# A relational graph layer: the first group of tiles in pairs, an earlier weight load, and the window table built in steps 1 to 3

## The reference

```python
h = relu(layernorm(x))                          # no gain, eps 1e-5
W_rel = einsum('rb,bdf->rdf', w_comp, weight)   # 32 types from 8 bases of 128 x 128
agg = segment_sum(h[src] * norm, etype * N + dst, R * N).reshape(R, N, D)
out = x + relu(einsum('rnd,rdf->nf', agg, W_rel) + h_bias + h @ loop_weight)
```

## Time and profile before

| | before |
|---|---|
| median of 3 runs | 1015.2 us |
| profiled execution | 1015.24 us |
| span of that execution | 1013.5 us |
| PE busy | 990.3 us (98%) |
| DVE busy | 955.0 us (94%) |
| ACT busy | 884.6 us (87%) |
| POOL busy | 723.8 us (71%) |
| mean granted clock of PE | 0.999 |

### The profile page before, as it was taken

One profiled execution on the slowest core, in us unless ns is written; L12 is line 12 of the kernel. 1 busy time (PEld: TensorE's weight loads), 2 busy tenths in 40 slices (PEclk: granted clock), 3 DMA queues, 4 the chain that ended last, 5 costly groups with the idle time before them and its releaser, 6 DMA issues.

```text
span 1013.5 us, 23775 instructions
## 1 busy us (share of the span) xinstructions
PE 990.3 (98%) x4902; PEld 574.4 (57%) x4902; DVE 955.0 (94%) x4366; ACT 884.6 (87%) x3242; POOL 723.8 (71%) x1282
## 2 busy tenths in 40 slices
PE   5899999999999999999999999999999999999996
PEld 2355555555556565656565555555555655555655
DVE  6999999999999999999999999999999999999995
ACT  6898989898888889898989898989898988889884
POOL 6877777777777777777777777777777777777740
PEclk9999999999999999999999999999999999999999
DMA  4556555556556555565565555465655655555544
GB/s 116 145 135 165 149 156 164 156 144 169 143 152 173 140 154 161 152 166 155 143 173 141 154 162 158 138 178 140 168 152 152 166 148 155 159 155 141 156 123 140
DMA packets 178223, 154.47 MB, mean 152 GB/s; under 512 B 17781, under 2 KB 151213, under 8 KB 178077
## 3 DMA queue, kind: packets, MB, share of 16 engines
q1 hardware_dynamic: 157261, 101.40, 35.6%
q0 software_dynamic: 20384, 51.32, 19.7%
q10 hardware_dynamic: 432, 0.22, 0.1%
HBM read 101.31 MB, written 51.56 MB: 151 GB/s over the span
## 4 chain that ended last, share of the span: by engine, by line
PE 93%; DVE 2%; POOL 2%; issue 1%; ACT 1%; DMA 1%; DVEq 0%; ACTq 0%; POOLq 0%
PE y_ps L790 33%; PE y_ps L797 31%; PE win_ps L812 9%; PE win_ps L807 8%; PE hT_ps L876 4%; PE hT_ps L803 4%; PE mix_ps L868 1%; POOL xg L578 1%; DVE sum_a L1019 1%; DVE sum_b L1019 0%; DMA xg<-x,idx 0%; DVE msg L1052 0%; PE y_ps L812 0%; DMA src_all<-src 0%; PE y_ps L807 0%
## 5 line engine op out<-in xcount | busy, mean ns | idle before, releaser
L578 POOL DMA_INDIRECT xg<-x,idx x392 | 382.0, 974 | 73.4 <-issue 34.0
L790 PE MATMUL y_ps<-w_all,hT 128*128 128x512 f32 x784 | 412.3, 608 | 2.9 <-DVE sum_a L1019 2.7
L797 PE MATMUL y_ps<-w_all,hT 128*128 128x512 f32 x784 | 400.3, 592 | 0.0
L523 POOL TENSOR_TENSOR u<-z 128x128 f32<-128x128 f32 x392 | 180.4, 460 | 182.8 <-ACT z L626 178.9
L626 ACT ACTIVATE z<-y_ps,mix 128x128 f32<-128x128 f32 x784 | 244.5, 366 | 44.8 <-PE y_ps L797 37.8
L1019 DVE SCALAR_TENSOR_TENSOR sum_b<-y_ps,mix,sum_b 128x128 f32<-128x128 f32 x784 | 265.8, 339 | 0.0
L797 PEld LDWEIGHTS y_ps<-w_all,hT 128*128 128x128 f32 x784 | 149.1, 190 | 187.9 <-issue 164.0
L790 PEld LDWEIGHTS y_ps<-w_all,hT 128*128 128x128 f32 x784 | 132.3, 189 | 119.1 <-DVE sum_a L1019 60.9
L622 ACT ACTIVATE z<-y_ps,mix 128x128 f32<-128x128 f32 x392 | 140.8, 359 | 63.6 <-issue 44.9
L660 ACT ACTIVATE hw<-xw,shift,nrstd 128x128 f32<-128x128 f32 x391 | 192.6, 494 | 0.4 <-DVE shift L1121 0.4
L1019 DVE SCALAR_TENSOR_TENSOR sum_b<-y_ps,mix,z 128x128 f32<-128x128 f32 x392 | 131.4, 335 | 36.1 <-issue 32.3
(11 more groups left out here) (107 smaller groups left out, 1174.3 us busy)
## 6 DMA issues: line engine op xcount, KB each, us to landing
seg<-msgs SPq DMA_DIRECT2D x391, 104.8 KB
msgs<-msg SPq DMA_DIRECT2D x98, 258.0 KB
xw<-x POOLq DMA_DIRECT2D x97, 256.0 KB
out<-res SPq DMA_DIRECT2D x97, 256.0 KB
xg<-x,idx POOLq DMA_INDIRECT x392
type_bc<-type_rows SPq DMA_DIRECT2D x52, 112.0 KB
w_all<-weight SPq DMA_DIRECT2D x1, 512.0 KB
type_bc<-type_rows SPq DMA_DIRECT2D x4, 80.0 KB
```

What stands on the lines that cost most here:

```text
L523: nc.gpsimd.tensor_tensor(u[:, r, :], z[:, r, 0, :], z[:, r, 1, :], ALU.add).then_inc(s_u, 1)
L578: nc.gpsimd.indirect_dma_start(xg[:, q, j, :], None, x, bass.IndirectOffsetOnAxis(ap=idx[:, q, j:j + 1], axis=0)).then_inc(s_gather[q * G ...
L790: nc.tensor.matmul(y_ps[2 * t % 5][:, :, :], hT[:, q, j, :], w_all[:, B // 2:B, :], start=True, stop=True).then_inc(s_y_high, 1)
L797: nc.tensor.matmul(y_ps[(2 * t + 1) % 5][:, :, :], hT[:, q, j, :], w_all[:, 0:B // 2, :], start=True, stop=True).then_inc(s_y, 1)
```

## The change

Group 0: each tile gets its negated mean at once (`s_mean_first` counts tiles). ACT computes three signs, applies relu to tiles 0 and 1, waits for their two transposes and copies them (`s_hT_first`, `s_hT_sb_first`), then comes the fourth sign, and relu of tiles 2 and 3, and a copy of these two. PE runs `first_tiles` within step 0: two transposes, the products of tile 0, two transposes, the products of tile 1; step 1 then begins with tile 2. The other four signs stand in ACT's steps 1 and 2, two in each.

Counts and table: `bin_counts(0)` stands at the head of DVE's step 1 and `bin_counts(1)` at the head of its step 3. `count_bins` is one sequence of eight matmuls in PE's step 3, after the products of the group's second tile. `row_table` stands in DVE's step 3, after the last slot and ahead of the next one-hot.

Loads: `w_all` is issued right after the first types, without a wait. The rest of `src_all` is issued after gather 3 has landed, ahead of `norm_all`, `dst_c` and the types.

```diff
--- before.py
+++ after.py
@@ -50,6 +50,8 @@
 SUMS_AT = 6
 OUT_AT = 5
 LATE = 4
+TABLE_STEP = 3
+PAIR = 2
 LAST_LOADS = 2
 MODE_STORE = 52
 SPAN = 8
@@ -268,6 +270,8 @@
         s_first_hot = sem("s_first_hot")
         s_bn_first = sem("s_bn_first")
         s_mean_first = sem("s_mean_first")
+        s_hT_first = sem("s_hT_first")
+        s_hT_sb_first = sem("s_hT_sb_first")
         s_dst = sem("s_dst")
         s_dst_c = sem("s_dst_c")
         s_consts = sem("s_consts")
@@ -391,10 +395,9 @@
             sp.dma_start(src_all[:, 0:FIRST], src[:, 0:FIRST]).then_inc(s_src_first, 16)
             sp.dma_start(norm_all[:, 0:FIRST], norm[:, 0:FIRST]).then_inc(s_norm_first, 16)
             load_type_rows(0, 0, 2, 0, s_types_first)
-            sp.dma_start(src_all[:, FIRST:NT], src[:, FIRST:NT]).then_inc(s_src, 16)
-            sp.wait_ge(s_gather[1], 16)
             sp.dma_start(w_all[:, :, :], weight.rearrange("b d f -> d b f")).then_inc(s_all, 16)
             sp.wait_ge(s_gather[G - 1], 16)
+            sp.dma_start(src_all[:, FIRST:NT], src[:, FIRST:NT]).then_inc(s_src, 16)
             sp.dma_start(norm_all[:, FIRST:NT], norm[:, FIRST:NT]).then_inc(s_norm, 16)
             sp.dma_start(dst_c[:, :], dst_cols).then_inc(s_dst_c, 16)
             load_types(0)
@@ -627,6 +630,10 @@
                 ins.then_inc(s_z, 1)
 
 
+            def sign(k):
+                nc.scalar.activation(signs[:, k, :], dst_f[:, :], ACT.Sign, bias=limits[:, k:k + 1], scale=-1.0,
+                                     accum_out=below_sum[:, k:k + 1]).then_inc(s_below, 1)
+
             def group_means(g, n, q):
                 if not is_before(g, RING):
                     act.wait_ge(s_hT, g - (RING - 1))
@@ -674,6 +681,10 @@
                 def mixing(j):
                     if 1 <= g <= NG:
                         scale_bases(g - 1, (q - 1) % RING, j)
+
+                def late_sign(i):
+                    if is_before(g, TABLE_STEP):
+                        sign(SPAN // 2 + 2 * (g - 1) + i)
 
                 def normalised(tiles):
 
@@ -702,6 +713,7 @@
                     window_std(g - STD_AT)
                 window(0)
                 mixing(1)
+                late_sign(0)
                 if here:
                     normalised(range(G // 2, G))
                 if node_group(g, TURN_AT) is not None:
@@ -717,6 +729,7 @@
                 if not beyond(g, NG - 1):
                     group_means(g + 1, round_after(n, q), (q + 1) % RING)
                 mixing(3)
+                late_sign(1)
                 if not beyond(g, NG - 1):
                     group_squares(g + 1, (q + 1) % RING)
                 window(3)
@@ -727,26 +740,24 @@
             act.wait_ge(s_consts, 1)
             nc.scalar.activation(root[:, :], eps_col[:, :], ACT.Sqrt)
             act.wait_ge(s_limits, 1)
-            def sign(k):
-                nc.scalar.activation(signs[:, k, :], dst_f[:, :], ACT.Sign, bias=limits[:, k:k + 1], scale=-1.0,
-                                     accum_out=below_sum[:, k:k + 1]).then_inc(s_below, 1)
-
             def first_relu(j):
                 nc.scalar.activation(h[:, 0, j, :], xg[:, 0, j, :], ACT.Relu, bias=neg_mean[:, 0, j:j + 1]).then_inc(s_relu, 1)
 
-            for k in range(SPAN - 2):
+            for k in range(SPAN // 2 - 1):
                 sign(k)
-            act.wait_ge(s_mean_first, 1)
-            first_relu(0)
-            first_relu(1)
-            sign(SPAN - 2)
-            sign(SPAN - 1)
+            for j in range(PAIR):
+                act.wait_ge(s_mean_first, j + 1)
+                first_relu(j)
+            act.wait_ge(s_hT_first, 1)
+            nc.scalar.activation(hT[:, 0, 0:PAIR, :], hT_ps[:, 0:PAIR, :], ACT.Copy).then_inc(s_hT_sb_first, 1)
+            sign(SPAN // 2 - 1)
+            act.wait_ge(s_mean_first, PAIR + 1)
+            first_relu(PAIR)
             act.wait_ge(s_mean, 1)
-            first_relu(2)
-            first_relu(3)
+            first_relu(G - 1)
             nc.scalar.activation(std[:, 0, :], nmv[:, NRING - 1, :, 1], ACT.Sqrt, bias=eps_col[:, 0:1]).then_inc(s_std, 1)
             act.wait_ge(s_hT, 1)
-            nc.scalar.activation(hT[:, 0, :, :], hT_ps[:, :, :], ACT.Copy).then_inc(s_hT_sb, 1)
+            nc.scalar.activation(hT[:, 0, PAIR:G, :], hT_ps[:, PAIR:G, :], ACT.Copy).then_inc(s_hT_sb, 1)
             group_means(1, 0, 1)
             group_squares(1, 1)
             sweep(act, STEPS, step, first=1)
@@ -771,15 +782,14 @@
         @block.tensor
         def _(pe):
 
-            def count_bins(half):
+            def count_bins():
                 counts = win_ps[0:1, :, :].rearrange("p b f -> p (b f)")
                 pe.wait_ge(s_first_hot, 1)
-                pe.wait_ge(s_bins, half + 1)
-                for k in range(half * (SPAN // 2), (half + 1) * (SPAN // 2)):
+                pe.wait_ge(s_bins, 2)
+                for k in range(SPAN):
                     mm = nc.tensor.matmul(counts[:, 0:BINS], in_bin16[:, k:k + 1], first_hot[:, SPAN - k:SPAN - k + BINS],
                                           start=k == 0, stop=k == SPAN - 1)
-                if half == 1:
-                    mm.then_inc(s_hist, 1)
+                mm.then_inc(s_hist, 1)
 
             pe.wait_ge(s_weights, 16)
 
@@ -838,16 +848,16 @@
 
             def step(g, n, q):
                 def messages(j):
-                    if 1 <= g <= NG:
-                        if j == 0:
+                    if 1 <= g <= NG and not (is_before(g, 2) and j < PAIR):
+                        if j == (PAIR if is_before(g, 2) else 0):
                             pe.wait_ge(s_hT_sb, g)
-                        if g == 1 and j == 0:
-                            pe.wait_ge(s_all, 16)
                         product_high(g - 1, (q - 1) % RING, j)
                         product_low(g - 1, (q - 1) % RING, j)
 
                 messages(0)
                 messages(1)
+                if g == TABLE_STEP:
+                    count_bins()
                 if node_group(g, TURN_AT) is not None:
                     window_transposes(g - TURN_AT)
                 if node_group(g, SUMS_AT) is not None:
@@ -868,7 +878,8 @@
                     nc.tensor.matmul(mix_ps[:, P:P + G * B], hotT[:, q, :], w_mix[:, :],
                                      start=True, stop=True).then_inc(s_mix_ps, 1)
                     if is_before(g, 1):
-                        count_bins(0)
+                        first_tiles()
+                        return
                     pe.wait_ge(s_relu, g * G + G)
                     if node_group(g, TURN_AT) is not None:
                         pe.wait_ge(n_hT_sb, g - TURN_AT + 1)
@@ -877,8 +888,24 @@
                     mm.then_inc(s_hT, 1)
                 messages(3)
 
+            def first_tiles():
+
+                for j in range(PAIR):
+                    pe.wait_ge(s_relu, j + 1)
+                    mm = nc.tensor.transpose(hT_ps[:, j, :], h[:, 0, j, :], ident[:, :])
+                mm.then_inc(s_hT_first, 1)
+                pe.wait_ge(s_hT_sb_first, 1)
+                pe.wait_ge(s_all, 16)
+                product_high(0, 0, 0)
+                product_low(0, 0, 0)
+                for j in range(PAIR, G):
+                    pe.wait_ge(s_relu, j + 1)
+                    mm = nc.tensor.transpose(hT_ps[:, j, :], h[:, 0, j, :], ident[:, :])
+                mm.then_inc(s_hT, 1)
+                product_high(0, 0, 1)
+                product_low(0, 0, 1)
+
             step(0, 0, 0)
-            count_bins(1)
             sweep(pe, STEPS, step, first=1)
 
             pe.wait_ge(s_table, 16)
@@ -1154,6 +1181,10 @@
                     if k is not None and j < windows_of(k):
                         window_stats(k, j)
 
+                if g == 1:
+                    bin_counts(0)
+                if g == TABLE_STEP:
+                    bin_counts(1)
                 tile_slot(g, n, q, 0, more)
                 stats_of(0)
                 tile_slot(g, n, q, 1, more)
@@ -1186,6 +1217,8 @@
                     window_rstd(g - STD_AT)
                 tile_slot(g, n, q, 3, False)
                 stats_of(3)
+                if g == TABLE_STEP:
+                    row_table()
                 if more:
                     one_hot(g + 1, (q + 1) % RING)
                 if node_group(g, STD_AT) is not None:
@@ -1204,17 +1237,12 @@
                 nc.vector.bn_stats(nstats[:, NRING - 1, j, :], xg[:, 0, j, :]).then_inc(done, 1)
                 dve.wait_ge(done, 2 * (j % DV) + 1)
                 nc.vector.bn_aggr(nmv[:, NRING - 1, j, :], nstats[:, NRING - 1, j, :]).then_inc(done, 1)
+                dve.wait_ge(done, 2 * (j % DV) + 2)
+                nc.vector.tensor_scalar(neg_mean[:, 0, j:j + 1], nmv[:, NRING - 1, j, 0:1], -1.0, None,
+                                        ALU.mult).then_inc(s_mean_first if j < G - 1 else s_mean, 1)
                 if j == 1:
-                    dve.wait_ge(s_bn, 2 * DV)
```

(7 more changed lines are left out.)

## The result

| | before | after |
|---|---|---|
| median, runs of one comparison | 1015.62 us (8 runs) | 1019.58 us (8 runs) |
| lowest to highest | 1015.01 to 1016.89 | 1017.81 to 1020.01 |
| ratio, 95% interval | | 1.0033 [1.0023, 1.0043] |
| profiled execution | 1015.24 us | 1018.22 us |

A forecast was written before the change was run, and what follows sets the result against it. Bound by POOL's queue to 31.77 us, DVE's to 62.59, then PE. Terms -0.7 (POOL's lead) + 0.34 + 2.49 (moved counts, table) + 0.1 (collision) = +2.2 on 1015.24 gave 1017.4 us, own range 1016.4 to 1019.3, 8 in 10: 1015.4 to 1019.2.

The forecast's parts named there:

- +4.1: Slow end of the summed terms: 0 + 2.83 + 0.44 + 0.8 us, giving 1019.3 us.
- 0.44 for the collision with POOL: Row table beside POOL's sums in step 3: SBUF collision costs DVE 0 to 0.44 us, taken as 0.1.
- What bounds it: POOL's queue to 31.77 us, DVE's queue to 62.59, then PE, full to the end.
- The head start: Group 0's start: first product near 12 us instead of 16.74, by itself worth nothing because POOL's queue sets u of tile 4.
- The moved table: bin_counts(1) and row_table in DVE's full stretch cost their whole length, 0.34 + 2.49 = 2.83 us, at least 2.63.
- POOL ahead by 0.7 us: POOL's waits before the gain and first u shrink: lead of 0 to 1.5 us, taken as 0.7.
- count_bins, signs, SP: Moved PE matmuls (rather 1.6 us), ACT signs and SP's window loads each cost 0; at most 0.8, 0.6 and 0.6 us.
- PE carries it unchanged to the end: After 62.59 us the summed +2.2 us passes through PE unchanged, giving 1017.4 us.
- A: Rival: the table finds room in DVE's full stretch, leaving only POOL's lead, 1014.5 us; chance 0.10.
- B: Rival: loads collide at the start, src_all late, POOL 1 us behind, 1019.2 us; chance 0.12.
- C: Rival: the products' head start of 4.7 us is kept whole, 1010.6 to 1013 us; chance 0.04.
- The rule of packet turns: DMA engines alternate rings by packet, so SP's loads little delay POOL's gathers; by it, POOL 1.5 us ahead, sum 0.8 less.

The follow-up runs named there:

- e1: Kernel before with only the counts and row table moved to steps 1 to 3, start and loads as before; 1019.85 us against 1015.64, ratio 1.0036.
- e3: Changed kernel with SP also waiting for gather 5 before issuing norm_all, dst_c and the types; 1016.96 us, ratio 1.0016 to the kernel before.
- e10: Changed kernel run again, unaltered; 1018.88 us against 1015.86 for the kernel before, ratio 1.0026.
- e8: e7 with the first two x loads issued by SP after gather 11 instead of by POOL; 1012.36 us, ratio 0.9966 to the kernel before.
- e9: e7 with group 0 started whole instead of in pairs; 1013.78 us, ratio 0.9981 to the kernel before.
- e11: e9 with e8's edit, so no pairs and first two x loads by SP; 1012.0 us, ratio 0.9963 to the kernel before.
- e2: Changed kernel with last four signs at the start, counts and table in step 1; 1015.2 us, ratio 0.9997 to the kernel before.
- e7: e3 with last four signs at the start, counts in step 1, table split into DVE's waits in steps 1 and 2; 1014.33 us, ratio 0.9984.
- e5: Changed kernel with twelve unused matmuls added on PE in step 4's wait; 1017.98 us against 1016.15 for the kernel before, ratio 1.0019.
- e6: Changed kernel with row_table's four operations spread over three places of step 3; 1017.82 us, ratio 1.0017 to the kernel before.
- e4: Changed kernel with both e2's and e3's edits; 1015.23 us, ratio 0.9993 to the kernel before.
- e12: Kernel before with only e8's edit, first two x loads issued by SP; 1014.57 us, ratio 0.9984.

## Why the prediction was right, and where its sizes were off

I predicted 1017.4 us from a base of 1015.24, with 1016.4 to 1019.3 as the likeliest case's own range and 1015.4 to 1019.2 as that of 8 in 10. The comparison gave 1019.58 beside 1015.62 for the kernel before, the second one 1018.88 beside 1015.86. In differences to before: +2.2 predicted, with +4.1 as the upper end; by medians +3.96 and +3.02 measured, by the ratios about +3.4 and +2.6. The direction and the way it comes about were forecast. That the size stayed under the upper end is in part luck: the +4.1 was made of 0.8 us for count_bins, which didn't come, and 0.44 for the collision with POOL, of which 0.17 came, while the clock's 1.4 to 1.6 us had no term.

- **What bounds it: right.** POOL's queue to u(4), DVE's own program to the sum ahead of tile 21, then PE full. PE is full from tile 21 on in all fourteen profiles. DVE is idle at most 0.4 us between its sum on u(4) and tile 21 in eleven of them, and 1.7 us in e1, e3 and e10, which is the step that failed, below. In e8, e9 and e11 DVE no longer waits for u(4), so its own program is the bound there already.
- **The head start is worth nothing by itself: right.** The first product came at 11.51 (I said near 12), 5.23 us early, and u(4) not at all (31.96 against 31.77). e9 and e11 show that taking the pairs out costs nothing.
- **The moved table is paid whole: right.** Its terms were 0.34 + 2.49 + 0.1 = 2.93 us; "between" grew by 2.88. It consists of bin_counts (38.45 to 38.69, 0.24 us) and the table (2.47 us), together 2.71 us; the hotT behind them took 0.59 us in place of 0.27, beside the issue of a gather on POOL, and the stretch as a whole grew by 0.17 us more than the 2.71. e2 and e7 show the inverse: where DVE waits for POOL, the same operations cost DVE nothing, though POOL's own queue got 0.4 us (e2) and 0.9 us (e7) longer between u(0) and u(4).
- **POOL ahead by 0.7 us: the mechanism right, the size not fixed.** u(0) was expected at 19.5 and u(4) at 31.1. The second trace of the same kernel has 19.43 and 31.13, the first 20.40 and 31.96: gather 5 took 3.19 us in one and 4.65 in the other, just over the upper bound of 4.59 that I had. In the first profile this term is +0.19 in place of -0.7, in the second -0.64. That 19.43 is so near to 19.5 is chance: the gain came at 14.77 and not 15.2, and u(0) waited 0.51 us for z, which I had at ready. I had bounded the gain between 0.4 us early and 1.0 us late, from one execution; the five profiles show 0.1 us early (14.77) to 1.4 late (16.24). My 384 KB beside the gather also left out dst_c (196 KB) and the types, which are issued there too. e3 shows the cause by moving the loads.
- **count_bins, signs, SP: right.** Eight matmuls took 1.52 us (I said 1.6). DVE waited for ACT's z once in the first profile, 0.23 us at 44.91. The windows' rows were there when POOL asked for them (rel, at 57.46), without a wait.
- **The step that failed: "PE carries it unchanged to the end".** I let the wait of 2.49 us on PE cost its length. Four profiled executions have that wait unfilled (after, e1, e3, e10), and in three of them the granted clock falls to its lower level right behind it; "between" is then 35.2 to 35.4 and not 33.8, 1.4 to 1.6 us more. PE's rows give the same price by themselves: from the first product behind the wait to the first one of the next tile are 2.43 us at the full clock (first profile), 3.89 in e1, 4.12 in e3 and 4.03 in e10, 1.5 to 1.7 us more. With that term e10 is -0.64 + 2.88 + 1.47 = +3.71 us at tile 21 (66.39 - 62.68), where the 1.47 is what "between" has over 33.79; the first profile is 0.19 + 2.88 = +3.07. Filling the wait (e5) or splitting it (e6) left no run above 1018.5. The Trainium skill, page "TensorE: Matmul & The Clock Gate", section "HAM oscillation — how this bites in real kernels", tells of the same mechanism in another kernel: waits for DMAs, longer than this one, let PE's clock drop, so that the next piece starts slow. The rows of e1, e3 and e10 agree, with 1.6 us as its price in e3; that of after, with the same wait and full clock, shows that it isn't certain.
- **Rivals.** A (a table hidden in DVE's stretch) needed 2.8 us of idle there; e6 shows that there is none. B (src_all late for POOL) didn't happen, since the row numbers of group 2 were copied at 14.27 without a wait; but what B had in mind, loads that collide, hit gather 5. C fell as argued.

The separation of the clock's share from POOL's rests on profiles, one for each kernel, and with three falls in four the two profiles without one (e5, e6) could be chance. The unprofiled runs speak for it but do not settle it. In e3 and e10 the profiled execution, with the fall, was the slowest of all runs of its kernel. By medians e5 and e6 lie 1.83 and 1.67 us over their kernel before, and the changed kernel and e1, which keep the wait in one piece, 3.96, 3.02 and 4.21; but the intervals of the ratios overlap (e5's reaches 1.0028, those of the changed kernel begin at 1.0023 and 1.0016), and the kernel before spreads nearly as widely without any such wait. So how often the clock falls in unprofiled runs stays open; the clock column of a whole run (0.993 to 1.0) is too coarse to tell, as e10 showed.

## What to carry to other kernels

Work that one engine does for nothing while it waits is only free there. To move it, look for the waits that the releasing queue leaves behind it (here DVE's for POOL in steps 1 and 2), put moved work ahead of such a wait, and shorten the queue that ends last (here POOL's, by the x loads that SP can issue). Then look at what it does to the engine that is waited for: beside DVE's scan POOL's own operations took longer, which is most of what e7's lead lost on its way to u(4). An early start of an engine that isn't that queue buys nothing. Price a new wait of PE by its length and by what its clock may lose after it, and cut it in two or fill it where the work can't be moved.

## What was not expected of the hardware

- Behind a wait of 2.49 us in step 4, PE's granted clock fell to 1.2 GHz in three profiled executions of four, at a cost of 1.4 to 1.6 us each; behind the waits of 2.47 us in e2 and 2.69 us in e4 two products were slow as well (1.84 to 1.91 us). Behind the wait of 1.51 us in e6 they stayed at 1.02 us. That is no safe length: in e6 and e10, near 23 us, two products took 1.73 to 1.92 us behind two shorter waits in a row (1.89 and 0.92 us, 1.81 and 0.92), and POOL then waited 0.25 and 0.27 us for z.
- At the start the same instructions ran at two speeds: the second product took 1.02 us before, 1.89 in e12 and 1.91 in e1, and in e9 and e11, which start alike, the third took 1.91 and 1.02. The profile's clock column shows 1.00 there in before and in e12 alike (18 to 20 us), so only the durations tell it. This is in line with another sentence of the Trainium skill (page "TensorE: Matmul & The Clock Gate", section "What's actually happening"): how many products run slow at the start differs between runs of one kernel.
- Beside three loads of 580 KB in all on another queue, a gather took 3.19 us in one execution and 4.65 in another. The rule of packet turns that the prediction cited from the Trainium skill (page "DMA: Bandwidth & Descriptors", section "Queues, rings and completion order") gives no such spread.
- DVE's scan, which reads two tiles of SBUF, held POOL up: the copy of row numbers took 0.86 or 0.87 us beside it in five profiles (after, e1, e3, e5, e10), ending with the scan, and 0.20 us in e6, where the scan stands elsewhere. The prediction priced this collision for DVE alone.
